# Attention denominators summed in four column tiles and spread by SBUF DMAs; residual tile built by an adding DMA

## The reference

```python
# mixer
low = x; highs = []
for _ in range(2):                       # two analysis levels, depthwise taps of length 4
    highs.append(dwconv(low, g_filter)[:, ::2]); low = dwconv(low, h_filter)[:, ::2]
# linear attention on the lowest band (1024 positions), 16 heads of 32 channels
q = k = elu(low) + 1; v = low
kv = einsum('bnhd,bnhe->bhde', k, v);  z = k.sum(axis=1)
num = einsum('bnhd,bhde->bnhe', q, kv)
den = einsum('bnhd,bhd->bnh', q, z)[..., None] + 1e-6
low = num / den
for h in reversed(highs):                # two synthesis levels
    low = dwconv(repeat(low, 2), h_synth) + dwconv(repeat(h, 2), g_synth)
m = layernorm(x + low) * gamma + beta
x = layernorm(x + m)
# feed-forward, integer weights of 1536x512, 1536x512, 512x1536, scaled by 1/127
x = layernorm(x + down(silu(gate(x)) * up(x)))
```

## Time and profile before

| | us |
|---|---|
| median of 3 runs (lowest, highest) | 1324.55 (1323.08, 1324.67) |
| the profiled execution | 1315.63 |
| span of its trace | 1313.8 |
| PE busy | 1248.6 (95%) |
| DVE busy | 980.5 (75%) |
| ACT busy | 684.3 (52%) |
| POOL busy | 373.6 (28%) |

### The profile page before, as it was taken

The page is one execution under the profiler, slowest core; times in us unless marked ns, Lnnn a source line. Parts: engine busy times, 40 slices in busy tenths (PEclk is TensorE's granted clock), DMA queues, the critical chain, the costliest instruction groups (busy, mean ns, idle before and its releaser), DMA issues.

```text
span 1313.8 us, 19451 instructions
## 1 busy us (share of the span) xinstructions
PE 1248.6 (95%) x6000; PEld 639.7 (49%) x6000; DVE 980.5 (75%) x1921; ACT 684.3 (52%) x1427; POOL 373.6 (28%) x794
## 2 busy tenths in 40 slices
PE   8899899989999999989999999999999999999998
PEld 6778444445444444445544444444444444445443
DVE  7888788968889599884889478955888388945241
ACT  6663563467435763457633664356434663366332
POOL 0303323044132441234330441234131432044101
PEclk9899899999999999999999999999999999999999
DMA  8880610016000230004200130004000410010000
GB/s 267 240 209 25 185 49 33 1 52 222 16 32 8 95 115 16 25 25 137 65 33 1 57 129 18 25 25 152 16 32 8 145 39 32 0 56 9 24 8 32
DMA packets 47269, 87.36 MB, mean 66 GB/s; under 512 B 8400, under 2 KB 24016, under 8 KB 46304
## 3 DMA queue, kind: packets, MB, share of 16 engines
q1 hardware_dynamic: 45472, 81.81, 19.2%
q0 software_dynamic: 1728, 4.72, 2.0%
HBM read 66.04 MB, written 25.19 MB: 69 GB/s over the span
## 4 chain that ended last, share of the span: by engine, by line
PE 31%; DVE 29%; issue 16%; ACT 10%; POOL 6%; DVEq 0%; ACTq 0%; POOLq 0%
DVE s_chan L1189 8%; DVE h_f L1552 6%; PE ps_down L593 6%; PE ps_down L594 6%; PE ps_gate L575 4%; PE ps_gate L576 4%; PE ps_up L576 4%; PE ps_up L575 4%; DVE hid L1558 3%; DVE low L1189 2%; ACT hid L1048 2%; DVE h_mem L1189 2%; ACT junk L839 2%; ACT h_f L1044 2%; DVE x L1331 1%
## 5 line engine op out<-in xcount | busy, mean ns | idle before, releaser
L593 PE MATMUL ps_down<-w,hid 128*128 128x512 f16 x768 | 293.8, 383 | 5.1 <-DVE z L1570 5.1
L575 PE MATMUL ps_gate<-x_hi,w 128*128 128x512 f16 x768 | 292.2, 380 | 5.4 <-ACT h_f L1044 2.6
L575 PE MATMUL ps_up<-x_hi,w 128*128 128x512 f16 x768 | 291.7, 380 | 3.3 <-DVE h_f L1552 3.3
L594 PE MATMUL ps_down<-w,hid 128*128 128x512 f16 x768 | 293.4, 382 | 0.0
L576 PE MATMUL ps_gate<-x_lo,w 128*128 128x512 f16 x768 | 292.1, 380 | 0.0
L576 PE MATMUL ps_up<-x_lo,w 128*128 128x512 f16 x768 | 291.6, 380 | 0.0
L1048 ACT ACTIVATE hid<-h_f 128x512 f16<-128x512 f32 x192 | 120.8, 629 | 241.3 <-DVE h_f L1552 241.3
L1552 DVE SCALAR_TENSOR_TENSOR h_f<-ps_up,h_f 128x512 f32<-128x512 f32 x192 | 131.8, 686 | 114.5 <-ACT h_f L1044 84.9
L1558 DVE TENSOR_TENSOR hid<-h_f,hid 128x512 f16<-128x512 f32 x192 | 138.7, 722 | 58.1 <-ACT hid L1048 57.3
L575 PEld LDWEIGHTS ps_up<-x_hi,w 128*128 128x128 f16 x768 | 75.3, 98 | 97.0 <-DVE h_f L1552 6.8
L593 PEld LDWEIGHTS ps_down<-w,hid 128*128 128x128 f16 x768 | 75.7, 99 | 94.0 <-issue 6.3
(11 more groups left out here) (249 smaller groups left out, 1868.1 us busy)
## 6 DMA issues: line engine op xcount, KB each, us to landing
xt<-x_tok SPq DMA_DIRECT2D x64, 256.0 KB, 2.7
out<-z SPq DMA_DIRECT2D x64, 256.0 KB, 2.0
xa<-x_chan SPq DMA_DIRECT2D x28, 515.0 KB, 5.7
xb<-x_chan SPq DMA_DIRECT2D x7, 2060.0 KB, 8.2
w<-weights POOLq DMA_DIRECT2D x12, 384.0 KB, 8.7
q_in<-q_scratch SPq DMA_DIRECT2D x7, 518.0 KB, 8.2
h_in<-h_scratch SPq DMA_DIRECT2D x7, 518.0 KB, 9.2
h_scratch<-h SPq DMA_DIRECT2D x7, 512.0 KB, 9.8
```

The source lines that it names most:

```text
L575: pe.matmul(ps_gu[k % 2][g][:, :], w, x1_hi[:, b, c, :], start=(c == 0), stop=False)
L593: pe.matmul(ps_d[t % 2][:, :], h_hi[:, k, t * P:(t + 1) * P], w, start=(k == 0), stop=False)
L594: mm = pe.matmul(ps_d[t % 2][:, :], h_lo[:, k, t * P:(t + 1) * P], w, start=False, stop=(k == NH - 1))
```

## The change

1. `z_heads` is 32 columns wide per chunk and `head_of` is one mask of 128 x 32, of which the first four columns hold the chunk's four heads. `dens` on PE writes chunk `c` to partitions `32c` to `32c+31` of `ps_y`, each product starting and stopping by itself, where four were added up before. `den` is 128 x 259, and DVE's two instructions on it cover 128 partitions.
2. `spread`, its matmul in each `attend`, and ACT's copy of its result are gone. SP waits for the reciprocal and issues four DMAs (chunks 2, 3, 0, 1), each of which reads the chunk's four rows of `den` and writes each to 32 partitions of `att`, which has a buffer for every chunk. DVE's multiplication waits for the matmul and for its DMA.
3. `beta_b` is gone. SP loads `beta` (from DRAM) into `xt` where it loaded `x`, and POOL, where it had the addition, waits for this load and issues a DMA that adds `x` to `xt`. `norm2` waits for this second DMA.
4. `norm3` of the first tile no longer waits for `att_done`, and `attend` 0 no longer waits for `den_step` and `x1_lo_ready`.

```diff
@@ SP
             def load_xt(j, t):
-                sp.dma_start(xt[:, t % 4, :], x_tok[bass.ds(j * TOK + t * P, P), :]).then_inc(ld_xt[t % 4], 16)
+                sp.dma_start(xt[:, t % 4, :], beta).then_inc(ld_beta[t % 4], 16)
...
+            def dens(j, batch, _):
+
+                hold(sp, den_step, 2 * (j + 1))
+                for c in (2, 3, 0, 1):
+                    rows = den[c * HEAD:c * HEAD + CHUNK_HEADS, :]
+                    sp.dma_start(att[:, c, :],
+                                 rows[:, None, :].to_broadcast([CHUNK_HEADS, HEAD, QW])).then_inc(ld_att[c], 16)
...
+            dens(0, 0, 0)
             hold(sp, set_dve, 1)
@@ PE
-                    mm = pe.matmul(ps_y[0:HEADS, 0:QW], z_heads[:, c, :], q_in[:, c, :], start=(c == 0),
-                                   stop=(c == NC - 1))
+                    mm = pe.matmul(ps_y[c * HEAD:(c + 1) * HEAD, 0:QW], z_heads[:, c, :], q_in[:, c, :],
+                                   start=True, stop=True)
...
             def attend(j, batch, c):
                 if c == 0:
-
-                    pe.wait_ge(den_step, 2 * (j + 1))
-
-                    pe.wait_ge(x1_lo_ready, SUBS * j)
                     pe.wait_ge(s_out, SUBS * j)
...
-                pe.matmul(ps_y[:, 0:QW], spread[:, c, :], den[:, :], start=True, stop=True)
@@ ACT
-            def attend(j, batch, c):
-
-                act.wait_ge(qk_ready, NC * j + c + 1)
-                act.wait_ge(syn2_step, N_SYN2 * (NC * j + c - 1))
-                nc.scalar.activation(att[:, c % 2, :], ps_y[:, 0:QW], ACT.Copy).then_inc(rden_out, 1)
@@ POOL
-                pool.wait_ge(ld_xt[t % 4], 16 * (2 * j + t // 4 + 1))
-                nc.gpsimd.tensor_tensor(xt[:, t % 4, :], xt[:, t % 4, :], beta_b[:, :], ALU.add
-                                        ).then_inc(x_beta, 1)
+                hold(pool, ld_beta[t % 4], 16 * (2 * j + t // 4 + 1))
+                nc.gpsimd.dma_start(xt[:, t % 4, :], x_tok[bass.ds(j * TOK + t * P, P), :], accum_op=ALU.add
+                                    ).then_inc(ld_xt[t % 4], 16)
@@ DVE
             def attend(j, batch, c):
-                dve.wait_ge(rden_out, NC * j + c + 1)
-                V.tensor_tensor(att[:, c % 2, :], ps_x[:, 0:QW], att[:, c % 2, :], ALU.mult).then_inc(att_done, 1)
+                dve.wait_ge(qk_ready, NC * j + c + 1)
+                dve.wait_ge(ld_att[c], 16 * (j + 1))
+                V.tensor_tensor(att[:, c, :], ps_x[:, 0:QW], att[:, c, :], ALU.mult).then_inc(att_done, 1)
```

More of the change, by code:

```diff
@@ L172, in mixer_ffn @@
         kv_blocks = sb("kv_blocks", [P, NC, P])
[L173 to L176, removed]
+        z_heads = sb("z_heads", [P, NC, HEAD])
+        head_of = sb("head_of", [P, HEAD])
+        den = sb("den", [P, QW])
         xb = sb("xb", [P, NC, XW])
@@ L185, in mixer_ffn @@
         low = sb("low", [P, 2, LW])
-        att = sb("att", [P, 2, QW])
+        att = sb("att", [P, NC, QW])
         xt = sb("xt", [P, 4, C])
@@ L226, in mixer_ffn @@
         ld_xt = [sem(f"ld_xt{n}") for n in range(4)]
+        ld_beta = [sem(f"ld_beta{n}") for n in range(4)]
         st_q, st_h2 = sem("st_q"), sem("st_h2")
@@ L400, in next_bands @@
                 load_bands(j, batch)
-            steps = {"low1": low1, "keys": keys_store, "norm2": after_norm2, "bands": next_bands}
+            def dens(j, batch, _):
[4 more added lines that the diff above has]
+                                 rows[:, None, :].to_broadcast([CHUNK_HEADS, HEAD, QW])).then_inc(ld_att[c], 16)
+            steps = {"low1": low1, "keys": keys_store, "norm2": after_norm2, "bands": next_bands, "dens": dens}
             def pro_h2_store(a):
@@ L420, in _ @@
                 load_xa(1, c)
-            for dst, src in ((mask[:, :], block_mask), (head_of[:, :, :], head_mask),
-                             (spread[:, :, :], head_spread), (edge_sb[:, :], edge),
-                             (gamma_b[:, :], gamma), (beta_b[:, :], beta)):
+            for dst, src in ((mask[:, :], block_mask), (head_of[:, :], head_mask),
+                             (edge_sb[:, :], edge),
+                             (gamma_b[:, :], gamma)):
                 sp.dma_start(dst, src).then_inc(ld_const, 16)
@@ L694, in pro_attend @@
                     pe.wait_ge(att_done, n - 1)
-                pe.matmul(narrow[:, 0:QW], spread[:, c, :], den[:, :], start=True, stop=True)
-                pe.matmul(wide[:, 0:QW], kv_blocks[:, c, :], q_in[:, c, :], start=True, stop=True
+                pe.matmul(bank[:, 0:QW], kv_blocks[:, c, :], q_in[:, c, :], start=True, stop=True
                           ).then_inc(qk_ready, 1)
@@ L724, in pro_low_band @@
                                                    (256, span_odd(half), (LOW_O, ATT_O))):
-                    todo = [(src, n, k) for src, part in zip((h2_in, att_pro), parts) for n, k in part]
+                    todo = [(src, n, k) for src, part in zip((h2_in, att), parts) for n, k in part]
                     for at_, (src, n, k) in enumerate(todo):
@@ L858, in norm3 @@
                                      ).then_inc(x1_hi_ready, 1)
-            early = {"low1": low1, "band2": band2, "high1": high1, "attend": attend, "synth2": synth2,
-                     "norm1": norm1, "norm3": norm3, "turn": turn}
+            early = {"low1": low1, "band2": band2, "high1": high1, "synth2": synth2, "norm1": norm1, "norm3": norm3, "turn": turn}
             late = {"exp": exp, "norm1q": norm1q, "normq": normq, "normx": normx}
```

63 lines of the change are left out of this document (27 added, 36 removed).

## The result

The changed kernel is slower: 1336.28 us (median of 5 runs, 1332.47 to 1339.66) against 1324.67 us (1323.08 to 1325.57) on the same chip, a ratio of 1.0095 with a 95% interval of 1.0076 to 1.0113. Forecast were 1310.5 us, with 0.14 for slower. The profiled execution took 1334.32 us, its span is 1332.5 us.

What follows compares the result with a forecast made beforehand. PE has hardly any idle time, yet DVE paces more than half of an iteration, so PE's savings count only on PE's chain. -8.8 - 5.5 - 2.7 + 3 = -14.0 us against the median 1324.55: 1310.5 us, range 1297 to 1328.

Steps and rivals of the forecast that it cites:

- step 1: Loop, attend 1 and 2: removing spread matmuls from PE's chain saves 1.26 us in each of seven iterations, 8.8 us.
- step 3: Loop: without POOL's addition DVE runs undisturbed, saving 5.5 us over three iterations with analysis, 0 in the others.
- those of `att` in the loop: Main loop: den is ready some 18 us ahead of the first attend, so the DMAs of att cost nothing.
- in the closing: Prologue's closing: DMAs of att land late behind busy traffic, a loss of 1.5 us, bounds 0 and 5.
- the copy: Loop, ACT: removing the copies of the spread's result gives 0, since ACT is not on the chain there.
- Step 2: Loop, dens on PE: the four column tiles count 0, since DVE paces that stretch.
- PE paces everywhere: Rival, 17%: all 28 loop spreads and the tiles count, no clock drops; -37 us at most, middle 1300.5 us.
- the saving turns into idle time: Rival, 17%: DVE paces 953.91 to 980.81 us too, so 8.8 us falls to about 2; 1321.4 us.
- the adding DMA is late: Rival, 13%: in iterations without analysis POOL's DMA lands behind other loads, losing 20 us over eight; 1330.5 us.
- Step 4: Prologue: -3.4 us from POOL's shorter issues, -0.8 from spreads, +1.5 from late DMAs of att; -2.7 us.
- Step 5: Loop, PE's clock: longer stalls cause two drops in four iterations, a loss of 3 us, bounds 0 and 7.

Runs made afterwards that it cites:

- e4: Kernel before with column tiles, no spread matmuls and DMAs for att reading 32 rows of den instead of 4, addition kept on POOL: 1319.59 us, 3.1 us below before.
- e2: Kernel before with the attention part alone (column tiles, no spread matmuls, DMAs for att from 4 rows), addition kept on POOL: 1333.95 us, 11.2 us above before.
- e5: Changed kernel with 32 rows of den instead of 4 for the DMAs of att: 1325.16 us, 2.4 us above before.
- e6: Changed kernel with 32 rows of den, and the adding DMAs of tiles 4 and 5 issued earlier, ahead of the xb load: 1315.07 us, 7.7 us below before.
- e12: Kernel before with every spread matmul of the loop issued twice: 1321.74 us, 0.6 us below before, ratio 1.0006.
- e3: Kernel before with den summed in four column tiles, spread matmuls and ACT's copies kept: 1321.83 us, 0.9 us below before.
- e8: Kernel before without the addition of beta, nothing replacing it: 1309.32 us, 13.4 us below before.
- e11: Kernel before once more, unchanged, one run for a second profile: 1323.59 us.
- e7: Changed kernel with 32 rows of den and descriptor space for POOL's DMAs of 2048 instead of 1024: 1321.88 us, 0.9 us below before.
- e10: Changed kernel, 4 rows of den, with the loop's DMAs of att issued in order 0, 1, 2, 3: 1331.51 us, 9.1 us above before.
- e1: Kernel before with the residual part alone (SP loads beta, POOL's DMA adds x): 1328.23 us, 5.5 us above before.

## Why the prediction was wrong, step by step

The sum had -14.0 us and the medians differ by +11.6. The largest saving, step 1's 8.8 us, was not there (some 1.7 us in e4's loop), while the one in the loop of step 3 was larger than said (9.7 us for 5.5). The sign was lost by three terms for the new DMAs: those of `att` in the loop, put at nothing, cost about 1.1 us in each of seven iterations (e2 against e4); in the closing, put at 1.5 us, 5.5 to 8.5 us; and the adding DMA's landing, put at nothing in the sum, 10.1 us (e5 against e6).

**Step 1, the spread matmuls on PE's chain (-8.8 us): wrong.** e4 has them removed and no other wait: 0.25 us per iteration, between block 0's end and block 1's start, and e12 has them doubled at no cost. PE did gain time: from the third down tile to `attend` 2, a stretch with one spread in it, it takes 17.71 us in e4 for 18.64 before (953.91 to 972.55). The rows are of the kernel before and of e4:

```profile
972.55 0.70 PE L519 MATMUL ps_y<-den,spread 16*128 16x259 f32 x2
```
```profile
959.66 0.39 PE L594 MATMUL ps_down<-w,hid 128*128 128x512 f16 x1 [1.58 <-DVE z L1558]
...
977.37 0.60 PE L521 MATMUL ps_x<-q_in,kv_blocks 128*128 128x259 f32 x2
```

But the stall ahead of that tile grew from 0.71 to 1.58 us, and at the end stands ACT, whose rows before (with one of POOL) and in e4 are:

```profile
968.13 0.63 POOL L1159 TENSOR_TENSOR rs<-rs,minus_part 128x1 f32<-128x1 f32 x1 [2.25 <-DVE z L1570]
...
971.57 0.81 ACT L1035 ACTIVATE z<-z,rs 128x512 f32<-128x512 f32 x1 [1.96 <-POOL rs L1114]
972.29 0.57 ACT L1044 ACTIVATE h_f<-ps_gate 128x512 f32<-128x512 f32 x1
```
```profile
977.03 0.81 ACT L1021 ACTIVATE z<-z,rs 128x512 f32<-128x512 f32 x1 [1.96 <-POOL rs L1100]
977.75 0.58 ACT L1030 ACTIVATE h_f<-ps_gate 128x512 f32<-128x512 f32 x1
```

ACT's `h_f` stands in its queue behind the scaling of `z`, which waits for POOL, which waits for DVE's `z`. DVE's wait of 1.50 us at 972.99, which I took for slack that "ends with PE", ended with this chain of small steps: from DVE's `z` (967.35 us, in e4 972.82) to this `h_f` it is 5.64 us in both kernels. Gapless PE was true; that PE paced was not.

By the rows even the 0.25 us are not PE's. A little earlier DVE waits for ACT's `low`, which before stood in ACT's queue behind the copy of `att`, 0.26 us after it; the copy had been put at 0. Before and in e4:

```profile
962.53 0.37 ACT L829 ACTIVATE att<-ps_y 128x259 f32<-128x259 f32 x1
962.79 0.91 ACT L774 ACTIVATE low<-h_in,coef 128x257 f32<-128x257 f32 x2
...
963.74 1.28 DVE L1189 SCALAR_TENSOR_TENSOR low<-h_in,coef,low 128x257 f32<-128x257 f32 x3 [0.39 <-ACT low L774]
```
```profile
969.21 1.28 DVE L1175 SCALAR_TENSOR_TENSOR low<-h_in,coef,low 128x257 f32<-128x257 f32 x3 [0.80 <-ACT low L773]
```

From the `z` of the third down tile on DVE (961.65, in e4 967.38 us) to this row it is 2.09 us before and 1.83 in e4, and this is the 0.26 us. No run removes the copy alone.

**Step 1, "den ready 18 us ahead, so the DMAs cost nothing": wrong.** I had allowed four times 2.7 us, 10.8 us for all four. They took some 22 us, at a share of 3.2 of 16 engines, in an order in which the loop's first chunk was third. It cost about 1 us in each of seven iterations (waits of 7.0 us) and, in e2, 7.0 us of loop.

**Step 2, the tiles (0): right**, by e3. With e12 it also refutes the rival that PE paces everywhere; the one by which the saving turns into idle time was right on step 1 (it had the 8.8 fall to about 2 us, and e4's loop gives 0.25 us in each of seven iterations). That the tiles run side by side was left open, and they do: 0.64 us for 1.93, a factor of 3.
The Trainium skill (TensorE: Matmul & The Clock Gate, Part 3: Packing small matmuls) had 2.38 for three tiles; for four this case shows 3.0.

**Step 3, the addition (-5.5 us in the loop, 0 without analysis): right in kind, too small.** e8 shows 9.7 us in the loop, since the 0.7 us at step 1 of block 1 counts in seven iterations; I had seen it at 974.38 and used it only as room for step 1. But the rival that I gave 13% took the gain back: **the adding DMA is late**. It lands 9.8 us after its issue in iteration 4, behind `xb`, and not the 2.7 us of a load from SP. By e6 against e5 its place costs 10.1 us. The rival's place and mechanism were right. Its price of 20 us was too high: tile 4 lands after 4.3 to 10.6 us and tile 5 after 7.4 to 8.6 us (4.2 in the last iteration), and only five of eight iterations have a wait.

**Step 4, the prologue (-2.7 us): wrong in its parts.** The issues take 0.9 us, not 0.56, and the fourth waits 4.11 us for room, so `h_in` came at 47.74 (before 45.64 us, 44.76 in e11) instead of at 40 us. ACT's wait grew from 8.42 to 9.28 us. With room (e7) `h_in` comes at 41.12, and ACT's wait is 4.41 us. The late `att` in the closing cost 5.5 us, 8.5 us in e2 and 8.1 us in e10, outside my bound of 5.
By the Trainium skill (DMA: Bandwidth & Descriptors, Why a DMA increments its semaphore by 16 and not by 1) and its 4 engines for 4 rows the loss would be nearer 5 than 1.5 us, and the measurement is on its side.

**Step 5, the clock (+3 us): did not come.** The stall ahead of `norm3`'s transposes kept its length:

```profile
1041.35 0.63 PE L560 MATMUL ps_y<-ident,x 128*128 128x128 f32 x4 [1.67 <-DVE x_lo L1339]
```

It was 1.72 us before, and 1.73 us in e4: PE's saving in `attend` 3 did not reach this stall. What takes it up on the way I did not follow. One stretch of 3.4 us at 1.2 GHz was added in the loop, at 322.43 us, just behind `norm2`'s wait of 4.70 us.

**The account.** Loop +9.4 (e1 +3.4 and e2 +7.0 give 10.4) and closing +5.5 are 14.9 us; the medians differ by 11.6. The second profile of the kernel before (e11), whose time is within 1.3 us of that kernel's median, tells where the rest is. Its last multiplication of the closing and that of the changed kernel (111.87 us, above) are

```profile
106.18 0.42 DVE L1430 TENSOR_TENSOR x<-ps_gate,x 128x259 f32<-128x259 f32 x1
```

From there to the first `h_f` it is 48.84 us in e11 and 44.36 us in the changed kernel, so 4.5 us come back behind the closing; ahead of its first multiplication the two differ by 0.2 us and behind the loop by less than 0.1: 0.2 + 5.5 - 4.5 + 9.5 = 10.7 us, which is the difference of the two spans. The three traces with 4 rows all have a short stretch there (44.4 to 45.7 us), the others 45.6 to 50.3 us. Whether a late closing always gives time back is not shown. Not separated either: how much of the adding DMA's median of 5.8 us (4.4 and 4.7 us for the two of e6 that are issued ahead of the traffic, against 2.6 us for SP's load of the same size) is the issue on POOL, the addition itself, or DVE.

## What to carry to other kernels

A work that moves from an engine to a DMA is free only if it lands in time where it stands: look at what is issued just behind it, and at how many rows each side of the DMA has, since 4 rows took over 5 us for what 32 rows do in a fraction of it. A gapless PE is no proof that PE paces: follow each wait on the engines that feed it through their queues, for an instruction may be held by the one ahead of it. And compare two traces by distances inside them, not by their spans.

## What was not expected of the hardware

- SP's four issues of `att` kept its queue for 9.18 us with 4 rows and for 2.57 us with 32, so a narrow DMA also holds up what stands behind it on the queue.
- POOL's issue of an adding DMA took 0.9 us, and with a descriptor space of 1024 three such DMAs of 256 KB were all that went out in a row: the fourth waited 2.2 to 4.1 us in the changed kernel. With 2048 four went out one behind the other without a wait (e7).
- Four products in column tiles of 32 columns took 0.64 us, where the same four took 1.93 us one after the other with weights of 16 columns: a factor of 3.0.
- Two executions of one kernel differed by 8.0 us in their first 150 us and by less than 0.1 us in the following 1037.
